# A graph network on one core: GpSimd's gathers by src kept within four groups of the steps that read them, two passes with pauses, last gathers and scatters in turn

## The reference

```python
def _L0_gnn_ref(x, edge_index, edge_attr, mW1, mb1, mW2, mb2, gW1, gb1, gW2, gb2, uW1, ub1, uW2, ub2, ln_g, ln_b):
    edge_input = jnp.concatenate([x[src], edge_attr], axis=-1)
    messages = _gelu(edge_input @ mW1 + mb1) @ mW2 + mb2
    gates = jax.nn.sigmoid(_gelu(edge_input @ gW1 + gb1) @ gW2 + gb2)
    aggregated = jax.ops.segment_sum(messages * gates, dst, num_segments=x.shape[0])
    combined = jnp.concatenate([x, aggregated], axis=-1)
    update = _gelu(combined @ uW1 + ub1) @ uW2 + ub2
    return layer_norm(x + update) * ln_g + ln_b

def _L1_gnn_ref(x, edge_index, edge_attr, Wq, bq, Wk, bk, We, be, Wv, bv):
    score = (x @ Wk + bk)[src] * (x @ Wq + bq)[dst] / sqrt(12) * (edge_attr @ We + be)
    score = jnp.exp(jnp.clip(score.sum(per head), -5.0, 5.0))
    msg = (x @ Wv + bv)[src] * score
    return segment_sum(msg, dst) / (segment_sum(score, dst) + 1e-06)

x = _layernorm(x + _L0_gnn_ref(x, ..., edge_attr_32, ...))
x = _layernorm(x + _L1_gnn_ref(x, ..., edge_attr_96, ...))
```

## Time and profile before

| what | value |
|---|---|
| median of 3 runs | 1965.96 us (1957.66 to 1973.78) |
| span of the profiled execution | 1985.4 us |
| PE busy | 1110.7 us (56%) |
| DVE busy | 944.9 us (48%) |
| ACT busy | 688.5 us (35%) |
| POOL busy | 936.1 us (47%) |
| DMA moved | 206.38 MB, mean 104 GB/s |

### The profile page before, as it was taken

One profiled execution on the slowest core, in us unless ns is written; L12 is line 12 of the kernel. 1 busy time (PEld: TensorE's weight loads), 2 busy tenths in 40 slices (PEclk: granted clock), 3 DMA queues, 4 the chain that ended last, 5 costly groups with the idle time before them and its releaser, 6 DMA issues. The chain is left out here.

```text
span 1985.4 us, 26381 instructions
## 1 busy us (share of the span) xinstructions
PE 1110.7 (56%) x5213; PEld 683.8 (34%) x5213; DVE 944.9 (48%) x4243; ACT 688.5 (35%) x1523; POOL 936.1 (47%) x978
## 2 busy tenths in 40 slices
PE   2211159993111389888989783120577752167784
PEld 1100025551000158776777672010233321023331
DVE  1000014441000038988789788000577761168886
ACT  0000015451000125776677567100343430034443
POOL 7777700006777340434333433777243357544444
PEclk9555559996555579999899886555888885589896
DMA  4222216662111033656455453222233331123341
GB/s 112 64 58 59 55 57 185 187 189 82 48 48 49 28 104 125 188 182 195 138 191 180 155 179 123 78 59 59 66 103 101 101 81 47 48 66 117 103 111 38
DMA packets 179806, 206.38 MB, mean 104 GB/s; under 512 B 110572, under 2 KB 124846, under 8 KB 179739
## 3 DMA queue, kind: packets, MB, share of 16 engines
q1 hardware_dynamic: 140709, 159.21, 25.8%
q0 software_dynamic: 31168, 45.88, 9.5%
q10 hardware_dynamic: 7862, 0.67, 0.3%
HBM read 101.29 MB, written 77.64 MB: 90 GB/s over the span
## 5 line engine op out<-in xcount | busy, mean ns | idle before, releaser
L460 POOL DMA_INDIRECT rows<-agg_d,dst_at x194 | 184.4, 951 | 335.7 <-DMA agg_d<-node_work 246.8
L441 POOL DMA_INDIRECT agg_d<-rows,put_at x196 | 188.3, 961 | 291.4 <-issue 253.9
L482 POOL DMA_INDIRECT out<-rows,put_at x196 | 190.8, 974 | 173.2 <-ACT rows L762 107.5
L475 POOL DMA_INDIRECT node_work<-agg_d,src_i x193 | 182.5, 946 | 183.7 <-DMA x_in<-node_work 126.8
L871 DVE SCALAR_TENSOR_TENSOR ps<-hidden,ps 96x512 f32<-96x512 f32 x49 | 33.9, 692 | 418.1 <-ACT hidden L706 309.6
L544 PE MATMUL ps<-hidden,mW2s 97*96 97x512 f32 x98 | 63.0, 729 | 293.9 <-issue 216.6
L432 POOL DMA_INDIRECT rows<-in_x,src_i x195 | 189.8, 973 | 63.2 <-issue 60.4
L624 PE MATMUL ps<-nT,Wks 96*96 96x512 f32 x98 | 68.1, 784 | 231.3 <-issue 126.3
L727 ACT ACTIVATE node_work<-node_work,nshift,nscale 128x96 f32<-128x96 f32 x392 | 145.5, 454 | 80.4 <-DVE nshift L995 70.6
L772 ACT ACTIVATE nT<-ps 96x512 f32<-96x512 f32 x99 | 56.3, 589 | 252.2 <-remote 167.3
L493 PE MATMUL ps<-ident,x_in 128*96 128x128 f32 x588 | 83.1, 278 | 86.7 <-DMA ea<-in_edge_attr 64.8
(11 more groups left out here) (152 smaller groups left out, 2471.1 us busy)
## 6 DMA issues: line engine op xcount, KB each, us to landing
agg_d<-zeros SPq DMA_DIRECT2D x40, 480.0 KB
x_in<-in_x SPq DMA_DIRECT2D x49, 384.0 KB
node_work<-agg_d SPq DMA_DIRECT2D x49, 384.0 KB
agg_d<-node_work SPq DMA_DIRECT2D x49, 384.0 KB
out<-node_work SPq DMA_DIRECT2D x49, 384.0 KB
mask<-cont_d SPq DMA_DIRECT2D x49, 208.0 KB
ein<-rows SPq DMA_DIRECT2D x49, 192.0 KB
mask<-cont_d SPq DMA_DIRECT2D x49, 192.0 KB
```

The lines of the kernel that those rows point to most:

```text
L441: pool.indirect_dma_start(agg_d, rows_at(put_at, g, j), rows[:, g * EJ + j, :], None).then_inc(agg_added[g % 2][j], 16)
L460: pool.indirect_dma_start(rows[:, g * EJ + j, :], None, x1_d, rows_at(dst_at, g, j)).then_inc(xd_gathered[g % 3][j], 16)
L475: pool.indirect_dma_start(ahead[:, g % AHEAD, j, :], None, x1_d, rows_at(src_i, g, j)).then_inc(x1s_gathered[g % 2][j], 16)
L482: pool.indirect_dma_start(out, rows_at(put_at, g, j), rows[:, g * EJ + j, :], None, bounds_check=N - 1, oob_is_err=False).then_inc(out_sca ...
```

## The change

All of it is in POOL's stream, but for two lines that only rename a semaphore of a memset. (1) In pass 1 group g waits until group g - 4 has been copied to `einT`. (2) Pass 2 waits once for all 49 `agg_copied` and not group by group, and a memset of `pause` (128x64, on POOL) follows each DMA. (3) In pass 3 such a memset follows each DMA too. Each memset waits for the one before it. (4) Passes 4 and 5 become one loop: the gather of group g waits until SP has taken group g - 4 (not g - 24), and after it comes the scatter of group g - 7.

```diff
+PAUSE = 64
+LEAD, BEHIND = 4, 7
...
+            def breathe():
+
+                n = next(pauses)
+                if n > 1:
+                    pool.wait_ge(rested, n - 1)
+                pool.memset(pause[:, :], 0.0).then_inc(rested, 1)
+
             for g in range(EGROUPS):
...
+                if g >= LEAD:
+                    pool.wait_ge(einT_copied, g - LEAD + 1)
...
             pool.wait_ge(zeros_stored, 16 * ZSTEPS)
+            pool.wait_ge(agg_copied, EGROUPS)
             for g in range(EGROUPS):
-                pool.wait_ge(agg_copied, g + 1)
                 for j in range(EJ):
...
                     pool.indirect_dma_start(agg_d, rows_at(put_at, g, j), rows[:, g * EJ + j, :], None).then_inc(agg_added[g % 2][j], 16)
+                    breathe()
...
                     pool.indirect_dma_start(rows[:, g * EJ + j, :], None, x1_d, rows_at(dst_at, g, j)).then_inc(xd_gathered[g % 3][j], 16)
+                    breathe()
...
-            for g in range(EGROUPS):
-                if g == AHEAD_FREE:
-                    for s in range(2):
-                        pool.wait_ge(out_stored[s], slot_total(s))
-                if g >= AHEAD:
-                    pool.wait_ge(x1s_loaded[(g - AHEAD) % XSLOTS], per_slot4(g - AHEAD, (g - AHEAD) % XSLOTS))
+            def gather_src(g):
+                if g >= LEAD:
+                    pool.wait_ge(x1s_loaded[(g - LEAD) % XSLOTS], per_slot4(g - LEAD, (g - LEAD) % XSLOTS))
...
-            for g in range(EGROUPS):
+            def scatter_out(g):
                 pool.wait_ge(fin_made, g + 1)
...
+            for g in range(EGROUPS + BEHIND):
+                if g < EGROUPS:
+                    gather_src(g)
+                if g == BEHIND:
+                    for s in range(2):
+                        pool.wait_ge(out_stored[s], slot_total(s))
+                if g >= BEHIND:
+                    scatter_out(g - BEHIND)
```

More of the change, by code:

```diff
@@ L19 @@
+import itertools
 from contextlib import ExitStack
@@ L47 @@
 AHEAD = 24
-AHEAD_FREE = 16
 AFIRST, ASTEPS = 7, 40
@@ L135, in build @@
         tail_a = sb("tail_a", [1, ASTEPS * 4], I32)
+        pause = sb("pause", [P, PAUSE])
         x_in = sb("x_in", [P, XSLOTS, NJ * D])
@@ L239, in build @@
         lnb_placed = sem("lnb_placed")
+        rested = sem("rested")
         tail_a_loaded, tail_a_fetched = sem("tail_a_loaded"), sem("tail_a_fetched")
         tail_x_loaded, tail_x_fetched, tail_x_placed = sem("tail_x_loaded"), sem("tail_x_fetched"), sem("tail_x_placed")
-        tail_loaded, tail_set, tail_gathered = sem("tail_loaded"), sem("tail_set"), sem("tail_gathered")
+        tail_loaded, tail_gathered = sem("tail_loaded"), sem("tail_gathered")
         x1s_loaded = [sem(f"x1s_loaded{s}") for s in range(XSLOTS)]
@@ L370, in _ @@
             sp.wait_ge(tail_loaded, 32)
-            sp.wait_ge(tail_set, 1)
+            sp.wait_ge(pads_set, 9)
             for t in range(2):
@@ L420, in rows_at @@
                 return bass.IndirectOffsetOnAxis(ap=index[:, g, j:j + 1], axis=0)
+            pauses = itertools.count(1)
+            def breathe():
[3 more added lines that the diff above has]
+                pool.memset(pause[:, :], 0.0).then_inc(rested, 1)
             for g in range(EGROUPS):
@@ L804, in _ @@
             dve.memset(group_dst[:, EGROUPS:], float(FAR)).then_inc(needs_step, 1)
-            dve.memset(tail_rows[:, :, :], 0.0).then_inc(tail_set, 1)
+            dve.memset(tail_rows[:, :, :], 0.0).then_inc(pads_set, 1)
             flat = lambda t: t[:, :, :].rearrange("p g j -> p (g j)")
```

## The result

The changed kernel took 1867.96 us (1856.16 to 1876.33), the kernel before 1963.52 us (1957.66 to 1973.78) in the runs beside it: a ratio of 0.955, interval 0.950 to 0.959. It is faster, as forecast, but 200 us slower than the predicted 1668 and outside the range. And that holds only on some chips at some hours, as the experiments brought to light: where the kernel before takes 1239 us, the same change costs 7.6%.

The account below looks back on a forecast made before the run. Waits bound the kernel, each indirect DMA holding the other engines for 1.41 us. Edge 400 + middle 608 + attend 672 + 5 for the ends = 1685 against 1985.4, so a median of 1668 us; range 1530 to 1840 for 8 in 10.

Parts of the forecast that it names:

- The edge stage: Pass 1 with its edge steps: 400 us instead of 725, at 7.39 us a step beside bursts of four DMAs.
- The middle stage: Passes 2 and 3 with the update stage: 608 us instead of 522, a loss of 86.
- spacing 1.25 + 0.22 = 1.47: Passes 2 and 3: each memset adds 0.22 us to POOL's 1.25 per DMA; POOL alone 573 us for 390.
- c = 0.49: Middle stage: each of some 374 DMAs costs the update steps 0.49 us, in 425 + 374c.
- the 1.41: All indirect DMAs: each holds something the engines need for 1.41 us; spaced closer, they build a backlog.
- Rival B: Pass 2: pauses don't keep the backlog down, spacing under 1.41; middle stage 710 us, total 1768; chance 0.20.
- an instruction between two DMAs has never less than its own start: Passes 2 and 3: argument against B, whose case was a 0.10 us memset hidden in the 0.30 gap.
- The attend stage: Passes 4 and 5: 672 us (585 to 755) instead of 736, with 41 steps of 13.5 us beside bursts of eight.
- `fin_made` has long come when it is asked for: Attend stage: the wait for `fin_made` of three groups back holds no gather.
- Rival C: Attend stage: a burst of eight is no worse than its parts, 11.3 us a step; total 1579 or 1530; chance 0.19.
- 792 in the middle stage: Middle stage: B with c = 0.98, named as the case beyond which the range's upper end, 1840 us, goes.
- queue of eight: GPSIMD's queue: if the stall were it running full, bursts of up to eight would be free of it.

Follow-up runs that it names:

- graded_e: Changed kernel with pass 2's memsets 64, 256, 512 and 1024 wide in its four quarters: 1796.2 us, beside 1966.2 for the kernel before.
- leadonly: Kernel before with one edit, pass 1 waiting for the copy to `einT` of group g - 4: 1239.3 us, ratio 0.9996, on a free chip.
- scatter512: Changed kernel with memsets 512 wide in pass 2 and none in pass 3: 1356.8 us, ratio 1.096 to the kernel before, free chip.
- nopause: Changed kernel without the memsets in passes 2 and 3: 1273.8 us, ratio 1.029 to the kernel before, on a free chip.

## Why the prediction was wrong

**The edge stage was right**: 378 us for the forecast 400, 7.04 a step for 7.39. That the mean came so near is luck in part, since POOL's bursts were eight and four by turns and not the forecast four. It is more than the whole of the gain in the traces: 725 - 378 = 347 us. By the same marks in both traces (last gather of pass 3, end of the last scatter) the middle stage went from 528 to 751 us and the attend stage from 730 to 725: 347 - 223 + 5 = 129 us.

**The middle stage failed**, 751 us for 608, and that is the step that missed the range. The term is "spacing 1.25 + 0.22 = 1.47", with the choice of c = 0.49 "since with pauses no backlog should form". The memset of 64 added 0.03 us, not 0.22, since it lies in the gap that follows a DMA anyway; the spacing of 1.29 is under the 1.41 that I had worked out myself, and pass 2 was a crawl with four update steps. Rival B is this case word for word, with its bound of "1.25 to 1.4". Even my 1.47 would not have been enough: graded_e shows 28.6 us a step there. A margin of 4% over 1.41 was none. Against B stood "an instruction between two DMAs has never less than its own start"; the trace says otherwise, the memset's 0.17 us adding 0.03.

**B was too cheap too**, 710 us where 751 came: 276 from the start of pass 2 to ACT's return at 654.0, as B has it, then 45 steps x 9.49 = 427 for B's 414, and 48 from the last Gelu at 1081.2 to the last gather of pass 3 (1128.3 + 0.95). The 20 that I gave the end should have been those 48; in the kernel before the same piece was as long (1204.8 to 1253.3).

**The attend stage**: 725 for 672. The start took 40 us from pass 4's first gather to the first Exp, not 20; the steps with gathers alone were cheaper than forecast (three, 22 us in all, for 41), the middle ones dearer (40 x 14.9 = 595 for 554), those with scatters alone took 45 for 36, and the end 23 for 21. Where bursts of eight stood by themselves, as from 1214.2 to 1254.6, a step took 13.5 us, the very forecast, which was the middle between two bounds that no row settled, and so luck. What the forecast lacked are the runs of 16. The sentence that `fin_made` has long come when it is asked for was wrong: POOL waits 219 us for it, in 35 places, the gathers behind stand with it, and then two groups' DMAs follow in one run, beside which a step takes about 22 us. What that wait cost in all no run shows. Rival C is out: eight by themselves cost (13.5 - 7.62) / 8 = 0.73 us each, four 0.32 to 0.65 ((8.90 - 7.62) / 4 and (10.21 - 7.62) / 4).

**The range** missed because B and the high end of the attend stage came together: 378 + 751 + 725 = 1854. I had given B a time with everything else at its middle, and put the end of the range by single cases. The upper end doesn't even hold the case that it names: 792 in the middle stage gives (400 + 792 + 672 + 5) x 0.990 = 1850, not 1840.

**What no view of the profile before could tell** is that the crawl isn't the kernel's own. On a free chip POOL is the bound of the kernel before, and every edit there that made POOL wait or added to its stream cost time (the lead did not, since its waits were met when they were reached). There the change is a loss (1.076) where the forecast has a gain.

The Trainium skill's rule on who shares ports (SBUF — State Buffer, Who interferes with whom) was set aside for ACT's gaps of 9.91 us. Those alone don't settle it, since ACT may stand still behind a DVE that is locked out; but ports shared by the same instructions would be shared on every chip, and on free chips DVE and ACT run undisturbed beside the same 41 DMAs. The Trainium skill's queue of eight (Advanced Engine Details and Errata, Engine Queue Depths), read as the prediction reads it, would have made bursts of eight free; they cost 0.73 us per DMA, more than bursts of four.

**Open** stays what is held for 1.41 us, and why on some chips at some hours only. POOL's DMAs look the same in both kinds (37.80 us for 41). Nor are the transfers slower: by the pages, the packets of the queue of indirect DMAs took 9.5% of 1985.4 us in the kernel before on a held chip and 15.9% of 1240.0 in leadonly on a free one, that is 189 and 197 us of all 16 DMA engines, those of SP's queue 25.8% and 42.3%, 512 and 525 us. Whether something else ran on the held chips at that hour is not on record. Not tried on a held chip: wide pauses in both passes 2 and 3, which by graded_e's steps should take the 24 us steps of pass 3 away too; scatter512, nopause and leadonly fell on free chips both times, so how much of the 0.955 each part gives (the lead above all) is read from the stages of the traces alone, and that the pauses of 64 gave nothing there is argued (ACT is free at 654 us; 196 DMAs of 1.41 us from 378 end at 654 with or without them), not shown by a run.

## What to carry to other kernels

Where a pause is to relieve something, work out the rate at which that thing is served (here 1.41 us per DMA, from the end of the stall and not from the end of the stream), measure what the pause adds net of the gaps that are there anyway, and leave a real margin: at 1.47 a step still took 28.6 us, at 1.68 it took 9.1. Before tuning against a stall that no wait explains, time the same kernel on other chips: an edit that holds the busiest engine back can be a gain where the stall exists and a loss where it doesn't. The one to keep is one that costs nothing on a free chip (here the lead of four groups, ratio 0.9996) and gains on a held one, which for the lead the edge stage of the traces says (725 to 378 us) and no run of it alone has shown. A wait added to each of many small instructions also takes its sequencer's running ahead, which here, on a free chip, was dearer (47 us) than the instructions (11 us).

## What the runs showed of the hardware

The same kernel took 1239 us on chips 3, 11, 12, 15 and 10, and 1964 to 1979 us in the recorded runs, on chip 6, and on chip 10 an hour later. In the second kind the other engines nearly stop beside indirect DMAs at 1.26 to 1.41 us (an edge step of 50 us for 5.0, an update step of 80 us for 8.9) and are free again when 1.41 to 1.42 us per DMA have passed; the crawl is still there at 1.47 (28.6 us) and all but gone at 1.68 (9.1 us). An instruction of DVE that has begun takes its usual time even then (0.69 us at both ends of rows 7); it is the starts that come late. POOL itself, with a memset behind each DMA, falls back to a mean of 1.408 and 1.411 us, where without memsets it issued a scatter every 1.26 us beside engines that stood still. On a free chip a memset of 128x64 behind each DMA adds 0.03 us to the spacing, since it lies in the gap that is there anyway.
